# Second score pass of the 256-token attentions: its last 28 products issued by fours over six banks

## What is computed

```
scores = jnp.einsum('bhqd,bhkd->bhqk', q, k) / np.sqrt(HEAD_DIM)
attn = jax.nn.softmax(scores, axis=-1)
out = jnp.einsum('bhqk,bhkd->bhqd', attn, v)
out = out.transpose(0, 2, 1, 3).reshape(B, S, D)
return out @ ow + ob
```

## Time and profile before

| | |
|---|---|
| median of 3 runs | 3420.77 us (3413.17 to 3423.53) |
| profiled execution | 3429.57 us, of which span 3427.1 us |
| mean granted TensorE clock | 0.855 of full speed |
| busy: PE, VectorE, ScalarE, POOL | 77%, 60%, 41%, 55% of the span |
| second pass, first to last matmul, l2a | 1418.6 to 1723.9 us |
| the same, l3f1a | 1848.0 to 2148.8 us |
| the same, l3f2a | 2926.9 to 3227.8 us |

### The profile page before, as it was taken

One profiled execution on the slowest core, in us unless ns is written; L12 is line 12 of the kernel. 1 busy time (PEld: TensorE's weight loads), 2 busy tenths in 40 slices (PEclk: granted clock), 3 DMA queues, 4 the chain that ended last, 5 costly groups with the idle time before them and its releaser, 6 DMA issues. The chain is left out here.

```text
span 3427.1 us, 69229 instructions
## 1 busy us (share of the span) xinstructions
PE 2652.1 (77%) x24514; PEld 1705.9 (50%) x24514; DVE 2054.0 (60%) x6095; ACT 1401.2 (41%) x2956; POOL 1886.7 (55%) x2224
## 2 busy tenths in 40 slices
PE   3439966878994568899998999562888886999872
PEld 2228854557881436555565555451333333555462
DVE  6852335762335553688626885315999998788413
ACT  2202213321223134366533665225666761566333
POOL 4767762674772212599831143574788785123364
PEclk8679987879997779799887997685999997899686
DMA  9208972214985730110001011222121210111133
GB/s 373 70 9 203 224 184 47 87 58 124 225 215 178 216 142 2 21 20 16 9 1 24 20 35 43 59 68 97 50 99 50 87 62 13 19 27 32 40 87 97
DMA packets 222726, 294.16 MB, mean 86 GB/s; under 512 B 36704, under 2 KB 179583, under 8 KB 216288
## 3 DMA queue, kind: packets, MB, share of 16 engines
q1 hardware_dynamic: 168544, 245.65, 23.2%
q0 software_dynamic: 47616, 39.44, 6.1%
q10 hardware_dynamic: 6272, 5.24, 0.6%
HBM read 181.88 MB, written 107.12 MB: 84 GB/s over the span
## 5 line engine op out<-in xcount | busy, mean ns | idle before, releaser
L4054 PE MATMUL l3am_y<-l3am_hc,ident 128*128 128x512 f32 x512 | 286.1, 643 | 77.0 <-DVE l3am_hc L3943 76.8
L3714 POOL TENSOR_TENSOR l3am_db<-l3am_du,l3am_bs 128x512 f32<-128x512 f32 x256 | 318.3, 1274 | 46.2 <-DVE l3am_hh L3935 45.4
L3935 DVE TENSOR_TENSOR_SCAN l3am_hh<-l3am_dA,l3am_db 128x512 f32<-128x512 f32 x256 | 300.0, 1209 | 20.4 <-ACT l3am_dA L3844 11.0
L1181 POOL TENSOR_TENSOR l2a_pT<-l2a_pT,kept 128x512 int32<-128x512 int32 x224 | 278.7, 1280 | 60.5 <-ACT l2a_pT L1387 60.5
L1268 DVE CUSTOM_DVE_ANT_0 l2a_junk<-l2a_s,addend 128x256 f32<-128x256 f32 x512 | 187.9, 421 | 63.3 <-PE l2a_s L1504 58.4
L3006 POOL DMA_INDIRECT l0f_table<-l0f2e_y,l0f2e_idx x128 | 178.9, 1398 | 81.7 <-DVE l0f2e_idx L2978 33.4
L3006 POOL DMA_INDIRECT l0f_table<-l0f1e_y,l0f1e_idx x128 | 179.5, 1403 | 65.5 <-issue 31.7
L1834 POOL DMA_INDIRECT l0f_rows<-l0f1r_row,l0f1r_idx x160 | 164.3, 1027 | 73.2 <-issue 51.1
L4054 PEld LDWEIGHTS l3am_y<-l3am_hc,ident 128*128 128x128 f32 x512 | 95.7, 200 | 204.9 <-DVE l3am_hc L3943 142.8
L1261 DVE TENSOR_REDUCE l3f2a_mx<-l3f2a_s 128x2 f32<-128x512 f32 x256 | 165.7, 685 | 46.5 <-PE l3f2a_s L1504 44.1
L1261 DVE TENSOR_REDUCE l3f1a_mx<-l3f1a_s 128x2 f32<-128x512 f32 x256 | 165.4, 685 | 44.8 <-PE l3f1a_s L1504 42.5
(11 more groups left out here) (821 smaller groups left out, 6874.2 us busy)
## 6 DMA issues: line engine op xcount, KB each, us to landing
l3am_bs<-l3a_b SPq DMA_DIRECT2D x32, 1024.0 KB, 6.5
l0f1m_w<-in_L_ffn_expert_w SPq DMA_DIRECT2D x64, 384.0 KB, 3.3
l0f2m_w<-in_L_ffn_expert_w SPq DMA_DIRECT2D x64, 384.0 KB
l0f_rows<-blank SPq DMA_DIRECT2D x8, 1930.0 KB, 22.3
l0f1m_w<-in_L_ffn_expert_w SPq DMA_DIRECT2D x64, 192.0 KB, 3.5
l0f2m_w<-in_L_ffn_expert_w SPq DMA_DIRECT2D x64, 192.0 KB
l1a_top<-l1a_kernel SPq DMA_DIRECT2D x12, 1024.0 KB, 11.9
l3f_rows<-blank SPq DMA_DIRECT2D x8, 1440.0 KB, 11.9
```

The costliest lines, as they stand in the source:

```text
L1181: self.nc.gpsimd.tensor_tensor(t, t, self.kept[:, f // 8 % 2, :].unsqueeze(1).to_broadcast([P, 2, 2 * P]), ALU.mult).then_inc(self.cut_g, 1)
L3714: G.tensor_tensor(db[j][n % 2][:, :], du[j][k % 2][:, :], bs[s // QUARTER][:, s % QUARTER, :], ALU.mult).then_inc(db_ready[j], 1)
L3935: V.tensor_tensor_scan(hh[j][n % 2][:, :], dA[j][n % 2][:, :], db[j][n % 2][:, :], 0.0, ALU.mult, ALU.add).then_inc(h_ready, 1)
L4054: T.matmul(yb[j][:, :], c.ident[:, :], hc[j][n % 2][:, :], start=(s == 0), stop=(s == N - 1)).then_inc(summed, 1)
```

## The change

The products 228 to 255 of the second pass are called late. They are no longer issued in the slots. At every even step the four products of this step and the next are issued at once behind the slots: q = 0 of all four, and then q = 1 of all four. Four successive products stand in four different row strips. Their banks are the three score banks and the three `e` banks in turn, so a late product waits for the product six before it to leave its bank; the first three wait for the maxima of the last three first-pass products instead. ScalarE and VectorE read the bank that `prob_bank` names. Nothing is added to or left out of what is computed, and no other engine's order changes.

```diff
+    def late(self, f):
+        return 16 * self.NB - 2 * self.LEAD <= f < 16 * self.NB
+
+    def prob_bank(self, f):
+        if not self.late(f):
+            return self.eb[f % 3]
+        t = f - (16 * self.NB - 2 * self.LEAD)
+        return (self.sb_[(16 * self.NB + t) % 3] if t % 6 < 3 else self.eb[f % 3])
...
     def pe_probs(self, pe, f, q):
...
-        if q == 0 and f >= 3:
-            if self.on_vector(f - 3):
-                pe.wait_ge(self.hidden, self.by_vector(f - 2))
+        t = f - (16 * self.NB - 2 * self.LEAD)
+        if q == 0 and 0 <= t < 3:
+            pe.wait_ge(self.mx_ready, 16 * self.NB - 2 + t)
+        elif q == 0 and f >= 3:
+            at = f - (6 if self.late(f) else 3)
+            if self.on_vector(at):
+                pe.wait_ge(self.hidden, self.by_vector(at + 1))
             else:
-                pe.wait_ge(self.p_ready, f - 2 - (self.by_vector(f - 3) if self.kept is not None else 0))
+                pe.wait_ge(self.p_ready, at + 1 - (self.by_vector(at) if self.kept is not None else 0))
         rows = slice(32 * i, 32 * i + 32)
-        m = self.nc.tensor.matmul(self.eb[f % 3][:, 2 * P * q:2 * P * q + 2 * P],
+        m = self.nc.tensor.matmul(self.prob_bank(f)[:, 2 * P * q:2 * P * q + 2 * P],
...
-        if self.inside(g - 1):
+        if self.inside(g - 1) and not self.late(g - 1):
             self.pe_probs(pe, g - 1, 1)
...
-        if self.inside(g):
+        if self.inside(g) and not self.late(g):
             self.pe_probs(pe, g, 0)
+
+    def pe_four(self, pe, g):
+        if self.late(g):
+            for q in range(2):
+                for k in range(4):
+                    self.pe_probs(pe, g + k, q)

     def pe(self, pe, weights, others=None):
...
                 self.pe_slot(pe, g + 2 * self.LEAD, g)
+            if u % 2 == 0:
+                self.pe_four(pe, 2 * e)
```

More of the change, by code:

```diff
@@ L1189, in dve_hide @@
         self.nc.vector.tensor_tensor(self.pT[f % self.NP][:, :].rearrange("p (h s) -> p h s", h=2),
-                                     self.eb[f % 3][:, :].rearrange("p (h s) -> p h s", h=2),
+                                     self.prob_bank(f)[:, :].rearrange("p (h s) -> p h s", h=2),
                                      self.addend[:, f // 8 % 2, :].unsqueeze(1).to_broadcast([P, 2, 2 * P]),
@@ L1386, in act_probs @@
             a.wait_ge(self.pv_done, (f - self.NP) // 4 + 1)
-        self.nc.scalar.activation(self.pT[f % self.NP][:, :], self.eb[f % 3][:, :], ACT.Exp).then_inc(self.p_ready, 1)
+        self.nc.scalar.activation(self.pT[f % self.NP][:, :], self.prob_bank(f)[:, :], ACT.Exp).then_inc(self.p_ready, 1)
     def act_sums(self, a, n):
```

## The result

The changed kernel takes **3366.09 us** in the median (3356.33 to 3370.35, four runs); the kernel before took 3422.15 us beside it (3413.17 to 3426.47, four runs). The ratio is **0.984**, 95% interval 0.981 to 0.987: 56 us less. 3376 us was forecast, with 3354 to 3401 as the range.

The account below looks back on a forecast made before the run. TensorE was taken to bound the tails, at half clock with two strips idle, and POOL's cuts to limit l2a too. Gains of 11 (l2a) + 17 + 17 (l3 stages) = 45 us gave 3420.8 - 45 = 3376 us, range 3354 to 3401.

Parts of the forecast that it names:

- The bursts: l3 tails from product 236 on: five four-strip bursts replace 21.3 us by 10.0 at half clock, saving 11.3 us.
- The slower rival: Tail bursts: strips reading one operand take turns, 6.8 us a burst at half clock; 3466 us, chance 0.04.
- pairs: Tail bursts: strips run in pairs, as before, giving no change; chance 0.07 together with the gain being hidden.
- The handover: Start of l3 tails: first bursts gain nothing, a weighing starts 2.1 us later, the next burst gives 2.0 back; net zero.
- The wait of block 15: l3 tails: TensorE waits once more while ScalarE copies `acc` between two blocks' weighings, costing 1 us.
- The clock: l3 tails: clock falls at the handover and returns near 2116, saving 7 us more per stage; coming back had 0.63.
- my best case: Clock never falls in l3 and returns early in l2a: 22 or 23 us per l3 tail, 12 for l2a; 57 us.
- the stretch behind 2116: Rest of the l3 tail after the clock returns: about 15 us at full clock instead of 22 at half.
- The rule that would have had no clock gain: Clock follows how busy TensorE recently was; small waits then bring no faster clock, 10 us per l3 stage, not 17.
- ScalarE: l3 tails at full clock: ScalarE sets the pace, 8.7 us of exponentials and some 2 of copies for 16 products.
- The floor: l3 tails bound by ScalarE throughout: 15.1 us of exponentials plus some 12 of other work; best case, 3364 us.
- l2a: l2a tail: nothing gained until 1688, then POOL's 19 cuts allow 12.4 us at most, half clock 9.3; 11 taken.

Follow-up runs that it names:

- the run with the loads behind: Changed kernel with the loads of the experts' first weights held back until the attention's last exponentials are done; one run, 3694.74 us.
- spare-products run: Kernel before, with 28 first-pass products computed once more in the tail, results unused, so interleaved steps go on in four strips; ratio 0.9925.
- the copy moved: Changed kernel with ScalarE's copy of the routing's transposes at the l3 handover moved behind exponentials 227 and 228, ratio 0.985; also on a combined version, 0.982.
- the root moved: Changed kernel with l2a's variance root on VectorE (L143) moved from block 14 to behind the last block; one run, 3711.20 us, l2a's tail 36.1 us.
- bursts by product: Changed kernel with each product's two matmuls, which share a strip, issued one after the other inside a burst; ratio 0.989.

## Why the prediction was right, and what it had wrong

**The bursts: right.** Priced 2.01 us at half clock and 1.08 at full from the earlier trace rows. At full clock l3f1a has 1.07. A whole burst at half clock stands in the run with the loads behind: 2.02 us (2360.07 to 2362.09, clock 0.50). The slower rival (strips that read one operand run in turn, decisive from 4.0 us on) did not happen, nor pairs.

**The handover: right.** The weighing that waits for ScalarE's copy starts 5.7 us behind the last first-pass record, where it was 4.3 (2098.04 from 2092.3, 2104.37 from 2100.1): 1.5 us later, 2.1 forecast, and the burst gives it back. The wait of block 15 was put at 1 us and is 0.81.

**The clock: the step that failed, by its size.** "It falls at the handover, where TensorE waits 2 to 3 us, and comes back near 2116": 14 us at half clock. The wait came, 2.25 us. In l3f1a the clock stayed at 1.00 through it, and in l3f2a it was down for some 4 us. So the l3 tails lost 25.6 and 24.1 us where I had 17; my best case had 22 to 23. The fall itself was well forecast, and l3f1a is the exception: nine traces here have the wait of 2.25 us at both handovers, and behind 17 of these 18 waits the clock was at half, for 3 to 7 us. The step that failed is how long it stays down: 14 us were put in, none and some 4 us were measured.

The error came from reading l2a as typical: there a wait stood before 0.50, but behind it came two-strip work, and the same stage now, with a longer wait (4.15 us), was back at 1.00 by 1700. In the kernel before, TensorE's wait at l3f1a's handover is only 0.55 us:

```profile
2103.25 1.18 PE L1521 MATMUL l3f1a_e<-l3f1a_qk 32*128 32x256 f32 x6 [0.55 <-ACT l3f1a_pT L1387]
```

The clock falls at 2105 all the same and is at half for the 47 us that are left. The spare-products run has the same handover, with 0.54 us, and the clock stays at 1.00 through it. With the old steps four strips had 0.89 to 0.91 over the tail where two have 0.55. So it was the two-strip work far more than the wait that kept the clock down.

A second term gave too little as well: for the stretch behind 2116, 22 us at half clock, the prediction adds up 13 us at full clock and then takes 15, with no reason given for the 2 us between.

**The rule that would have had no clock gain: not borne out.** The Trainium skill (TensorE: Matmul & The Clock Gate, The HAM clock gate) ties the clock to how busy the engine has recently been. With busy read from the records this case does not bear it out: 10.00 of 10.00 us busy at 0.50. The 1.96 of 4.00 at 1.00 above says less, as TensorE had been busy right before it and the same wait mostly did bring the clock down. The number of strips at work at once fits the tails; what the chip counts is not shown.

**ScalarE: half right.** It was to set the pace at full clock; it is busy 18.90 of 26.20 us and TensorE 22.40. The floor was put at 27 us, with ScalarE's work in a row, and the tails are 26.2 and 27.7.

**l2a: right.** 11 us were forecast, and the next stage starts 10.6 us earlier (1816.7 to 1806.1). The tail alone gave 12.2, near the 12.4 that POOL's 19 cuts allowed at most; the head took 2.6 back. The small instruction stayed at 9.44 us, and the cuts behind it came in a row but for one gap of 1.02 us. That cuts set this end is shown by removing four of them.

**The sum.** 45 us forecast, 56 measured: 11 for l2a was right, and 34 for the l3 stages should have been nearly 50. The range held the 3366 us because its lower end lay below the best case of 3364. The heads, which differ by up to 3 us between the two traces, were not in the sum. The gain is smaller on the other chips (50 us by the medians, of 3749) because the l3 tails are 33 us there.

## What to carry to other kernels

Where a stage starts or ends with one of two interleaved passes alone, look at how many strips are at work: the clock can stay at half with TensorE's records unbroken, so the idle strips cost twice. Batch independent products until all strips have work, and pay for it with banks that the other pass no longer uses; then see which engine is next (here POOL's cuts in one stage, VectorE's maxima at the other end). Removing one short wait that ScalarE causes is worth trying, but measure the end of the stage and not the wait.

## What the runs showed of the hardware

- **The clock and the strips.** Two strips of four, records without a gap: 0.50. Four strips, in the same place, with or without useful work: 1.00 for most of the time. Behind a wait of 2.25 us the clock fell to half in 17 of 18 cases, for 3 to 7 us with four-strip work; in one it stayed at 1.00. With the copy moved the wait is 0.22 or 0.23 us, and in those four cases it stayed at 1.00 there.
- **The order within a burst.** With two matmuls for the same strip in a row a burst took 1.10 us against 1.07 where nothing else held it, and 1.47 to 1.71 in four of eight; why those were longer is open.
- **A small VectorE instruction against a row of POOL's.** L143 handles 128x16 elements and takes 0.17 us when POOL does nothing. Beside POOL's cuts it took 5.76 to 9.47 us and ended with POOL's row in all 14 traces: 1688.09 with 1688.06 before, 1690.52 with 1690.49 after, 1988.09 with 1988.06 with the root moved. The Trainium skill (SBUF — State Buffer, SBUF: two separate sides) describes a port pair that VectorE and GpSimd share as an exclusive lock, held for a whole instruction; these ends agree with one blocking the other, but the block lasts through a row of many cuts, not one of 1.28 us. VectorE's other instructions (hides, maxima) ran beside the same cuts.
- **A standstill without a reason in the profile.** On two chips ScalarE stands for 3.3 to 3.5 us at one exponential of l3f1a's tail, the same one in all seven kernels that ran there with its order as in the changed kernel. On the first chip it does not, nor in the kernel with bursts by product on a fourth; but with the copy moved it stands there for 3.66 us on that fourth chip too. With the copy moved it also stands for 5.86 and 5.79 us at an earlier exponential, and TensorE then stands for 3.40 and 3.36 us. The causes were not found.
